# Layer 0 state space: time-step sums and output-matrix weighing on GpSimd, and layer 1's modulation columns at unit 9

## The reference

```python
x_dbl = xp @ Wx.T
dlt, Bp, Cp = jnp.split(x_dbl, [dt_rank, dt_rank + N], axis=-1)
delta = jax.nn.softplus(dlt @ Wdt.T + bdt)          # time step
A = -jnp.exp(A_log)
# for each state n of 16:  h_t = exp(delta_t * A_n) * h_(t-1) + delta_t * B_t,n * x_t
# y = sum over n of C_n * h_n
return y + xp * Dp
...
return y * jax.nn.silu(z) @ Wo.T
...
x = x + ga * _L0_attn_ref(h, ...)                   # ga: gate of the modulation, one row per sequence
```

## Time and profile before

| | us |
|---|---|
| median of 3 runs | 1180.49 |
| lowest, highest | 1177.71, 1180.70 |
| span of the profiled execution, first to last instruction | 1175.1 |
| median less that span | 5.4 |
| busy in the span: PE, DVE, POOL, ACT | 878.0, 887.3, 738.3, 630.2 |
| end of the state-space stage (gate of the last column half) | about 505 |

### The profile page before, as it was taken

One profiled execution on the slowest core, in us unless ns is written; L12 is line 12 of the kernel. 1 busy time (PEld: TensorE's weight loads), 2 busy tenths in 40 slices (PEclk: granted clock), 3 DMA queues, 4 the chain that ended last, 5 costly groups with the idle time before them and its releaser, 6 DMA issues. The chain is left out here.

```text
span 1175.1 us, 14982 instructions
## 1 busy us (share of the span) xinstructions
PE 878.0 (75%) x4244; PEld 565.5 (48%) x4244; DVE 887.3 (76%) x1790; ACT 630.2 (54%) x1401; POOL 738.3 (63%) x508
## 2 busy tenths in 40 slices
PE   7797769886987787753999736596987978349930
PEld 4243324334433433333999713264665767339920
DVE  4896999899979999966666555486896878465512
ACT  4787635874587465516343313656567684246710
POOL 0898799989988999702666376355433443037646
PEclk8999989998999898865999967598989977569975
DMA  6644445455544554340233312111101020142323
GB/s 185 184 131 131 125 147 166 137 157 160 162 131 143 164 164 156 113 164 13 71 85 87 72 50 68 45 34 50 45 2 64 28 74 19 54 165 73 71 63 98
DMA packets 90905, 118.95 MB, mean 101 GB/s; under 512 B 12508, under 2 KB 48804, under 8 KB 90696
## 3 DMA queue, kind: packets, MB, share of 16 engines
q1 hardware_dynamic: 84168, 104.34, 28.7%
q0 software_dynamic: 6656, 13.64, 5.0%
HBM read 103.70 MB, written 14.25 MB: 100 GB/s over the span
## 5 line engine op out<-in xcount | busy, mean ns | idle before, releaser
L687 POOL TENSOR_TENSOR ma_bu<-ma_u,ma_row_b 128x1024 f32<-128x1024 f32 x128 | 300.7, 2377 | 15.6 <-DVE ma_u L898 8.0
L416 PE MATMUL y_ps<-ma_h,ident 128*128 128x512 f32 x512 | 254.1, 635 | 27.4 <-POOL ma_h L697 23.1
L1215 POOL DMA_INDIRECT s_rows<-xs,take x112 | 128.9, 1151 | 162.3 <-POOLq L951 105.6
L563 ACT ACTIVATE decay_ps<-ma_delta,negA 128x512 f32<-128x512 f32 x256 | 172.5, 686 | 85.8 <-DVE ma_h L790 82.9
L416 PEld LDWEIGHTS y_ps<-ma_h,ident 128*128 128x128 f32 x512 | 100.4, 204 | 156.1 <-issue 111.1
L1568 POOL TENSOR_TENSOR mi_dec<-mi_dec,mi_gm 128x512 f32<-128x512 f32 x32 | 40.7, 1272 | 135.0 <-DVE mi_gm L2033 111.5
L1232 PE MATMUL s_up_ps<-s_xt,s_w 128*128 128x128 f32 x896 | 122.6, 282 | 1.2 <-ACT s_xt L1259 1.2
L780 DVE TENSOR_TENSOR_SCAN decay_ps<-decay_ps,ma_carry,ma_bu 128x512 f32<-128x512 f32 x88 | 110.1, 1271 | 12.6 <-issue 9.7
L790 DVE TENSOR_TENSOR ma_h<-decay_ps,ma_row_c 128x512 f32<-128x512 f32 x176 | 116.9, 665 | 0.0
L1232 PEld LDWEIGHTS s_up_ps<-s_xt,s_w 128*128 128x128 f32 x896 | 113.2, 198 | 1.6 <-DVE s_w L1291 1.0
L697 POOL TENSOR_TENSOR ma_h<-ma_h,ma_row_c 128x1024 f32<-128x1024 f32 x40 | 97.1, 2428 | 17.4 <-DVE ma_h L780 15.6
(11 more groups left out here) (323 smaller groups left out, 1766.0 us busy)
## 6 DMA issues: line engine op xcount, KB each, us to landing
ma_row_b<-bc_rows SPq DMA_DIRECT2D x128, 256.0 KB, 3.6
ma_row_c<-bc_rows SPq DMA_DIRECT2D x128, 256.0 KB, 3.3
mi_cs<-cs_rows SPq DMA_DIRECT2D x32, 256.0 KB
ys<-s_outs SPq DMA_DIRECT2D x28, 256.0 KB
w<-in_experts SPq DMA_DIRECT2D x1, 4112.0 KB, 14.9
w<-in_experts SPq DMA_DIRECT2D x1, 3072.0 KB, 10.3
xs<-rows SPq DMA_DIRECT2D x4, 512.0 KB, 3.4
out<-X SPq DMA_DIRECT2D x8, 256.0 KB
```

What stands on the lines that cost most here:

```text
L416: mm = pe.matmul(y_ps[:, j, :], m.ident[:], h[g % HS][:, j, :], start=False, stop=True, skip_group_check=True)
L563: act.activation(decay[s % DS][:], delta[b % 2][:, j, col(c)], ACT.Exp, scale=m.negA0[:, j, n:n + 1]).then_inc(decay_done, 1)
L687: pool.tensor_tensor(bu[g % BUS][:], u[b % 2][:, :, col(c)], both(row_b[g % BS]), ALU.mult).then_inc(bu_done, 1)
L1215: pool.indirect_dma_start(rows[s % ROWS][:], None, m.xs[layer], bass.IndirectOffsetOnAxis(ap=m.take[:, s:s + 1], axis=0)).then_inc(fetched ...
```

## The change

All seven time-step sums but that of the very first column half go from VectorE to GpSimd, at the same unit numbers. The first one stays on VectorE and has a semaphore of its own (first_delta), so that each semaphore counts one engine. The four weighings of the output matrix go to GpSimd and to units 17 to 20. The piece "columns" is made by TensorE at unit 9 instead of 12, and read by ScalarE a unit later in each case.

```diff
-    ROWS, STORE_ROWS, LOAD_ROWS, WEIGH_OUT, FIRST_MOD, LAYER1 = 3, 11, 13, 18, 12, 4
+    ROWS, STORE_ROWS, LOAD_ROWS, WEIGH_OUT, FIRST_MOD, LAYER1 = 3, 11, 13, 17, 9, 4
...
+        def delta_ready(engine, b, c):
+            if b + c == 0:
+                engine.wait_ge(first_delta, 1)
+            else:
+                engine.wait_ge(delta_done, 2 * b + c)
...
         @block.gpsimd
         def _(pool):
+            def make_delta(b, c):
+                d = delta[b % 2][:, :, col(c)]
+                pool.wait_ge(ln_done, 2 * b + c + 1)
+                pool.tensor_tensor(d, d, u[b % 2][:, :, col(c)], ALU.add).then_inc(delta_done, 1)
...
+            def weigh_out(b):
+                pool.wait_ge(rows_moved, 16 * 2)
+                pool.tensor_tensor(wo[:, b], m.wo0[:], m.gate[:, 0, 0, b, :].unsqueeze(1).broadcast_to([P, HALVES, P]),
+                                  ALU.mult).then_inc(wo_done, 1)
...
+                if g == FIRST_SUM:
+                    make_delta(0, 1)
                 if g == FIRST_U:
                     make_u(0, 1)
...
+                if b + 1 < NBATCH and SUM <= s < SUM + 2:
+                    make_delta(b + 1, s - SUM)
                 if b + 1 < NBATCH and U <= s < U + 2:
                     make_u(b + 1, s - U)
+                if b == 0 and WEIGH_OUT <= s < WEIGH_OUT + NBATCH:
+                    weigh_out(s - WEIGH_OUT)
                 if g + LEAD < TOTAL:
                     make_bu(g + LEAD)
...
         @block.vector
...
-                    if b == 0 and s == FIRST_SUM:
-                        make_delta(0, 1)
-                    if b == 0 and WEIGH_OUT <= s < WEIGH_OUT + NBATCH:
-                        weigh_out(s - WEIGH_OUT)
...
-                    if more and SUM <= s < SUM + 2:
-                        make_delta(b + 1, s - SUM)
```

More of the change, by code:

```diff
@@ L167, in mamba @@
             sem(n) for n in "mod_done prep act_prep pool_prep xn_done rows_moved".split())
-        (piece_done, piece_read, silu_done, z_silu_done, soft_step, ln_done, delta_done, u_done, stored, bu_done,
+        (piece_done, piece_read, silu_done, z_silu_done, soft_step, ln_done, first_delta, delta_done, u_done, stored, bu_done,
          decay_done, scan_done, product_done, pool_product_done, acc_done, yg_done, out_done, x_done, wo_done,
@@ L171, in mamba @@
          pool_carry) = (
-            sem(n) for n in ("piece_done piece_read silu_done z_silu_done soft_step ln_done delta_done u_done stored "
+            sem(n) for n in ("piece_done piece_read silu_done z_silu_done soft_step ln_done first_delta delta_done u_done stored "
                              "bu_done decay_done scan_done product_done pool_product_done acc_done yg_done out_done "
@@ L547, in state_decay @@
                 if n == 0 and j == 0:
-                    act.wait_ge(delta_done, 2 * b + c + 1)
+                    delta_ready(act, b, c)
                 if s == 0:
@@ L675, in _ @@
         def _(pool):
+            def make_delta(b, c):
+                d = delta[b % 2][:, :, col(c)]
+                pool.wait_ge(ln_done, 2 * b + c + 1)
+                pool.tensor_tensor(d, d, u[b % 2][:, :, col(c)], ALU.add).then_inc(delta_done, 1)
             def make_u(b, c):
                 r = b % 2
-                pool.wait_ge(delta_done, 2 * b + c + 1)
+                delta_ready(pool, b, c)
                 pool.tensor_tensor(u[r][:, :, col(c)], delta[r][:, :, col(c)], xp(b, c)[:], ALU.mult).then_inc(u_done, 1)
@@ L796, in gate, with make_first_delta @@
                 dve.tensor_tensor(z, y_ps[:], z, ALU.mult).then_inc(yg_done, 1)
[L798 to L801, removed]
+            def make_first_delta():
+                d = delta[0][:, :, col(0)]
+                dve.wait_ge(ln_done, 1)
+                dve.tensor_tensor(d, d, u[0][:, :, col(0)], ALU.add).then_inc(first_delta, 1)
             def add_out(b, q):
@@ L864, in modulate_rows @@
                                                     ALU.mult))
[L866 to L869, removed]
             dve.memset(m.hT[:, :, 0:PAD], 0.0).then_inc(prep, 1)
@@ L895, in _ @@
             then_prep(dve.scalar_tensor_tensor(shift0[:, 2 * BT:], mean0[:, 2 * BT:], -1.0, rstd0[:, 2 * BT:], ALU.mult, ALU.mult))
-            make_delta(0, 0)
-            dve.wait_ge(delta_done, 1)
+            make_first_delta()
+            dve.wait_ge(first_delta, 1)
             dve.tensor_tensor(u[0][:, :, col(0)], delta[0][:, :, col(0)], xp(0, 0)[:], ALU.mult).then_inc(u_done, 1)
```

## The result

The changed kernel takes 1175.92 us (median of 20 runs, 1169.12 to 1182.33) against 1182.47 for the kernel before in the same group of runs; the ratio is 0.9949 (95% interval 0.9931 to 0.9967), by which it is 6.0 us less; microseconds of a ratio below are worked out in the same way. The measured time lies in the predicted range of 1168 to 1179 (forecast 1173.1, from a kernel before at 1180.49), and the direction is right. But the profiled execution shows a last gate only 2.8 us earlier, and it shows why the later terms of the sum came out otherwise.

What follows compares the result with a forecast made beforehand. VectorE and GpSimd, nearly balanced in the state-space stage, were taken as the bound. With 5.6 us at the first boundary, 1.7 at each of the next two and GpSimd's lag in batch 3, 7.4 us: 1180.49 to 1173.1, range 1168.0 to 1179.0.

Steps and rivals of the forecast that it cites:

- What bounds the kernel: State-space stage: VectorE and GpSimd near balance; GpSimd bounds batch 0's first half; gate at 173.71 has 1.2 us slack.
- The sum of unit 7: Batch 0, unit 7: the sum costs GpSimd 2.34 us, a held-up bu saves 1.89; net +1.1 us for GpSimd.
- the gain is eaten: Rival on GpSimd: longer weighings, no saving from held-up instructions or a logarithm wait; 1 to 3 us earlier, 1178.5; 10%.
- The prediction's other reading: Sum of unit 7: no saving from the held-up bu, term +2.3 us, forecast 1.2 us later.
- The columns: Unit 16: ScalarE's 3.89 us wait goes; less 1.1 us, VectorE starts 2.8 us earlier.
- The weighings: Four weighings: VectorE loses 6.9 us; GpSimd gets 0.75 us each, 3.0 us, bounds 2.9 and 4.7.
- First boundary: Batch 0 to 1: GpSimd's product of unit 29 ends at 160.1, adds take 7.98 us, gate at 168.1, 5.6 us earlier.
- Second and third boundary: Closing gates of batches 1 and 2: product 2.1 us later, adds at full clock in 5.40 us, gates 1.7 us earlier each.
- low-clock rival: Second and third gates: adds at 1.2 GHz take 7.98 us, each gate 0.9 us later; 3.8 us earlier overall, 1176.7; 15%.
- Batch 3: No sums; its gate at unit 18 follows GpSimd, 7.2 us early, VectorE 9.0; stage end moves by 7.4 us.
- The total: Whole kernel: span from 1175.1 to 1167.7, median from 1180.49 to 1173.1; the forecast itself has 47%.

Runs made afterwards that it cites:

- e1: The kernel before with only the modulation columns of layer 1 at unit 9 instead of 12; ratio 0.9983 to the kernel before.
- e9: The changed kernel plus zero-adding matmuls (fills) of 256 columns in all of TensorE's long waits; ratio 0.9834 to the kernel before.
- e5: The changed kernel itself once more, nothing altered, for a second trace; ratio 0.9949 to the kernel before.
- e6: The changed kernel plus zero-adding matmuls of 512 columns before the closing gates, 7 in batch 0, 3 each in batches 1 and 2; ratio 0.9875 to the kernel before.
- e12: The changed kernel with fills of 256 columns as in e9, but more of them where TensorE still waited; ratio 0.9866 to the kernel before.
- e8: As e4, plus fills of 512 columns in TensorE's long waits, which were too long; ratio 0.9928 to the kernel before.
- e10: As e4, plus fills of 256 columns in TensorE's long waits; ratio 0.9886 to the kernel before.
- e4: The changed kernel with all seven sums back on VectorE (weighings on GpSimd, columns at unit 9); ratio 0.9932 to the kernel before.

## Why the prediction was right, and where not

- **What bounds the kernel.** Right at the boundary of batches 0 and 1: the chain of GpSimd's product, adds, gate. Incomplete elsewhere: TensorE bounds the first half of batches 1 and 2 and the gate in the middle of batch 0, and I had not read its busy time by stretch.
- **The sum of unit 7.** Predicted 1.1 us net for GpSimd, measured 1.4 (the product of unit 8 starts at 79.35, 77.96 before). The held-up bu fell from 4.25 to 2.35 as expected; a wait of 0.84 us for ScalarE's logarithm came in, which is the start of the rival "the gain is eaten", and stopped there. The prediction's row was weak evidence on who was first: GpSimd's bu starts at 65.20 by the trace and VectorE's instruction (line 859) at 65.43, and the profile's spans on GpSimd are rough. In the changed kernel it was VectorE that was held up: the same instruction (line 881, at 66.52) took 1.50 us instead of 0.67 beside the sum that GpSimd had begun at 65.11. The prediction's other reading, with nothing saved (by the Trainium skill, SBUF — State Buffer, Who interferes with whom), would have been 2.3 plus the wait, 3.1.
- **The columns.** The scan of unit 16 came 2.4 us earlier in the changed kernel (2.8 predicted), and e1 shows the 3.89 exactly. But the gate at 111.45 gave back all but 1.0 of it, waiting for TensorE. The first boundary's sum was not hurt, because GpSimd bounded it.
- **The weighings.** 0.73 us each for a predicted 0.75; alone they moved the first gate by 6.7 for 6.6.
- **First boundary.** 5.66 us earlier, 5.6 predicted; by the means of two traces each 6.0. Two small errors cancelled in the first: the product ended 0.6 us earlier than forecast, and the adds took 8.44 instead of 7.98. VectorE waited 4.89 us for TensorE at this gate where about 7 were forecast.
- **Second and third boundary.** This term failed: "Here TensorE has transposes and logits up to the adds and I expect full clock, 5.40 us". The product ended at 275.67, 0.9 us behind the forecast, because the middle of the batch had lost 0.9 to slower matmuls, and the adds took 8.38 us. My argument against the low clock was that the wait of 4.13 us at the first gate had been longer; but idle times of 1.46 to 2.17 us were followed by 12 slow adds (6.89 to 8.38 us) in all six rows of these two gates in the changed kernel's two traces and in e9. It isn't a rule: at other places of e5, e6 and e12, 1.53, 1.77 and 1.75 us were followed by adds at full clock.
- **What the two halves of a batch took.** The term belongs to the second half, from the gate in the middle to the closing one. The kernel before took 54.56 or 54.57 us for it in batches 1 and 2 of both its traces, the changed kernel 55.99, 55.90, 55.65 and 54.41: on average 0.9 us more instead of 1.7 less, just what the low-clock rival had worked out for each gate. The first half took 59.17, 61.00, 61.57 and 61.02 us before and 60.11, 60.18, 59.19 and 59.39 after, 1.0 us less on average: there the changed kernel has the restart at full clock, for which the prediction had no term. The two cancel, and a batch took 115.3 us before and 115.2 after.
- **What the term was worth with the clock kept up.** With fills and the sums on VectorE (e8, e10) the second half took 54.57 us in all four rows, as before, and in e10 VectorE reached the closing gates last; with fills and the sums on GpSimd, and the adds at full clock (e12), it took 53.04 and 52.93, 1.6 us less for a predicted 1.7. So the mechanism was right and the clock was the wrong input. In e9, with the adds at 7.11 us, it took 54.71 and 54.63, no gain. (e12 and e10 don't have the same fills; that fills alone don't shorten this half is shown by e8 and e10.)
- **Batch 3.** Predicted was a third gate 9.0 us early and a last one 7.4, since GpSimd would lag. The stretch between the two is 102.0 us in nearly every kernel of the table (e6: 102.6), moved or not; that step isn't borne out. VectorE, not GpSimd, fills its first half: it is busy for 51.92 of the 52 us from 402 to 454, in the kernel before and in the changed one.
- **The total.** Predicted were 5.6 at the first boundary and 1.8 net behind it, 7.4; measured, by the means of the traces, 6.0 and 0.1. The low-clock rival, 3.8 us, had the mechanism and the size at the second and third gate right and no term for the restarts either. So the result lies between the two, and that it came within 1.4 us of my forecast is in part luck: behind the first boundary a loss that I had held for unlikely was made good by a gain that I had not seen.

Left open: how much of the changed kernel's 6.0 us is owed to the sums. With e4 at 8.0 and overlapping intervals, the times can't say if leaving them on VectorE is better; the traces say only that they cost 0.8 to 1.9 us at the first gate (166.14 in e4, 166.97 and 168.05 in the changed kernel) and save some 3 at TensorE's restart. Why the clock is low behind one idle time of 1.5 to 2 us and full behind another is open too.

## What to carry to other kernels

When work is moved between two balanced engines, ask for each stretch which engine is without waits there, TensorE included: what one stretch gains passes through the next only at that engine's pace, and at the clock that it is granted after its own wait. Where TensorE waits a few microseconds for a late operand and its matmuls are on the path, matmuls that add zeros can be worth more than moving elementwise work (here, by the ratios, 9 to 14 us on top of the change's 6 in e6, e9 and e12, and 5 us on top of e4 in e10); size them by a measured row, keep them shorter than the wait, and read two traces of each kernel before a term of 1 to 3 us is explained.

## What was not expected of the hardware

- TensorE's clock could be at 1.2 GHz after idle times as short as 1.46 to 2.17 us, and at 2.4 GHz after others of 1.75 and 1.32 us (the projection in 2.05). In the same code at the same place it differed from run to run: 12 adds in 8.36 and in 6.89 us behind waits of 1.68 and 1.46.
- With it the end of one 500 us stage moved by 4.6 us between two executions of the changed kernel, and by 2.0 us between two of the kernel before.
- A matmul of f32 with 512 columns appears as two records and takes 0.88 us, with 256 columns 0.45, at full clock, also when all that it adds is zero; in e12 the granted clock stayed at 1.00 across the second boundary with such fills in the waits.
